# Four layers of cross attention on one core: in the narrow layer, products issued for two key tiles at a time, with sixteen probability buffers

## The reference

```python
xn = rmsnorm(x, norm_w)
q = (xn @ wq).reshape(B, T, N_HEADS, HEAD_DIM)        # 16 heads of width 16
k = (cond @ wk).reshape(B, S, N_KV_HEADS, HEAD_DIM)   # 4 groups share keys and values
v = (cond @ wv).reshape(B, S, N_KV_HEADS, HEAD_DIM)
scores = jnp.einsum('btgrd,bsgd->bgrts', qg, k) * scale
attn = jax.nn.softmax(scores.astype(jnp.float32), axis=-1).astype(q.dtype)
out = jnp.einsum('bgrts,bsgd->btgrd', attn, v).reshape(B, T, N_HEADS * HEAD_DIM)
return residual + out @ wo
```

## Time and profile before

| | us |
|---|---|
| median of 3 runs | 5466.34 |
| lowest, highest | 5460.77, 5468.5 |
| span of the profiled execution | 5460.9 |
| TensorE busy in it | 5173.7 (95%) |
| VectorE busy | 3684.8 (67%) |
| ScalarE busy | 2245.5 (41%) |
| GpSimd busy | 2695.0 (49%) |
| score blocks of the narrow layer, L765, 832 matmuls | 335.9 |
| maxima's tiles, L744, 1024 matmuls | 415.0 |
| products, L786, 1664 matmuls | 380.8 |

### The profile page before, as it was taken

The page is one execution under the profiler, slowest core; times in us unless marked ns, Lnnn a source line. Parts: engine busy times, 40 slices in busy tenths (PEclk is TensorE's granted clock), DMA queues, the critical chain, the costliest instruction groups (busy, mean ns, idle before and its releaser), DMA issues.

```text
span 5460.9 us, 81559 instructions
## 1 busy us (share of the span) xinstructions
PE 5173.7 (95%) x21484; PEld 2708.9 (50%) x21484; DVE 3684.8 (67%) x5908; ACT 2245.5 (41%) x4042; POOL 2695.0 (49%) x2048
## 2 busy tenths in 40 slices
PE   7999999999979898987999999999989999999999
PEld 4455545554444444444455555555445455545554
DVE  6767676767667676765767666676676667676767
ACT  2433344334425455552444444344424444444443
POOL 1656565656510101011656566666625656565655
PEclk8999999999979999997999999999989999999999
DMA  2010101010020101001010101010011010101010
GB/s 72 14 27 14 27 14 27 14 27 14 14 43 15 24 16 23 16 15 26 14 26 13 26 13 26 13 26 19 8 28 24 16 26 13 26 13 26 13 26 17
DMA packets 40356, 116.57 MB, mean 21 GB/s; under 512 B 7350, under 2 KB 20150, under 8 KB 35068
## 3 DMA queue, kind: packets, MB, share of 16 engines
q1 hardware_dynamic: 39938, 112.04, 9.4%
HBM read 26.86 MB, written 2.10 MB: 5 GB/s over the span
## 4 chain that ended last, share of the span: by engine, by line
PE 82%; issue 7%; DVE 6%; DMA 2%; SPq 1%; ACT 0%; DVEq 0%; POOL 0%; ACTq 0%; POOLq 0%
PE OB L654 19%; PE SS L594 13%; PE ST L625 11%; PE ST L627 9%; PE ST L551 5%; PE ST L567 4%; PE OB L786 4%; DVE mpart L1087 4%; PE ST L765 3%; PE SS L744 3%; PE ST L572 3%; PE ST L672 3%; PE ZB L607 2%; DMA Q<-rawQ 1%; PE ZB L744 1%
## 5 line engine op out<-in xcount | busy, mean ns | idle before, releaser
L282 POOL TENSOR_TENSOR acc<-acc,P 128x512 f32<-128x512 f32 (+1 forms) x1776 | 2362.5, 1356 | 455.1 <-ACT P L934 308.8
L934 ACT ACTIVATE P<-ST 128x512 f32<-128x512 f32 (+1 forms) x2496 | 1385.5, 597 | 2012.0 <-PE ST L627 1703.7
L1087 DVE TENSOR_REDUCE mpart<-SS 128x1 f32<-128x400 f32 (+1 forms) x3072 | 1665.0, 563 | 764.1 <-PE SS L594 709.1
L654 PE MATMUL OB<-P,V 128*64 128x512 f32 (+1 forms) x4992 | 1348.0, 618 | 1.1
L594 PE MATMUL SS<-KS,Q 128*128 128x400 f32 (+1 forms) x3072 | 1171.6, 387 | 70.2 <-DVE mpart L1087 67.1
L625 PE MATMUL ST<-Q,K 128*128 128x512 f32 (+1 forms) x2496 | 1061.3, 425 | 32.9 <-issue 18.3
L594 PEld LDWEIGHTS SS<-KS,Q 128*128 128x128 f32 x3072 | 585.0, 192 | 860.0 <-DVE mpart L1087 758.5
L627 PE MATMUL ST<-Q,K 128*128 128x512 f32 (+1 forms) x2496 | 989.6, 396 | 0.0
L278 POOL TENSOR_TENSOR acc<-P 128x512 f32<-128x512 f32 x192 | 241.3, 1278 | 1410.8 <-ACT P L934 1310.8
L625 PEld LDWEIGHTS ST<-Q,K 128*128 128x128 f32 (+1 forms) x2496 | 462.8, 185 | 515.8 <-ACT P L934 348.3
L1106 DVE RECIPROCAL R<-ZB 128x64 f32<-128x64 f32 (+1 forms) x432 | 371.3, 860 | 408.9 <-PE ZB L607 408.9
(11 more groups left out here) (126 smaller groups left out, 3608.1 us busy)
## 6 DMA issues: line engine op xcount, KB each, us to landing
Q<-Q SPq DMA_DIRECT2D x48, 512.0 KB, 4.5
KS<-K SPq DMA_DIRECT2D x48, 400.5 KB, 3.8
K<-K SPq DMA_DIRECT2D x48, 400.5 KB, 5.3
Q<-Q SPq DMA_DIRECT2D x32, 256.0 KB, 4.3
wk<-in_wk SPq DMA_DIRECT2D x25, 256.0 KB, 4.4
wv<-in_wv SPq DMA_DIRECT2D x25, 256.0 KB, 4.6
Q<-rawQ SPq DMA_DIRECT2D x16, 256.0 KB, 3.8
wq<-in_wq SPq DMA_DIRECT2D x25, 128.0 KB, 4.3
```

The source lines that it names most:

```text
L282: eng.tensor_tensor(out, out, P[0:rows_of(t), u % NP, :], ALU.add).then_inc(done, raised)
L654: last = pe.matmul(OB[64 * jj:64 * jj + 64, :], V[0:k, t, 64 * b:64 * b + 64], P[0:k, (2 * s + jj) % NP, :], start=t == 0, stop=t == KT - 1)
L934: act.activation(P[0:k, u % NP, :], ST[u % 4][0:k, :], ACT.Exp, scale=SCALE).then_inc(act_p, 1)
L1087: dve.tensor_reduce(mpart[:, i // len(KCH), i % len(KCH):i % len(KCH) + 1], SS[i % 2][:, 0:w], AX.X, ALU.max).then_inc(dve_s, 1)
```

## The change

```diff
+GRUNS = (2, 2, 2, 2, 2, 3)
+GRUN_END = [sum(GRUNS[:i + 1]) - 1 for i in range(len(GRUNS))]
...
+        PX = sb("PX", [128, 7, 512])
...
-        PG = [P[:, i, :] for i in range(NP)] + [acc[:, i // 2, i % 2, :] for i in range(3)]
+        PG = [P[:, i, :] for i in range(NP)] + [acc[:, i // 2, i % 2, :] for i in range(3)] \
+            + [PX[:, i, :] for i in range(7)]
...
+                def weigh(t):
+                    k = rows_of(t)
+                    for j in range(JQ):
+                        last = pe.matmul(OB[j * QD:j * QD + QD, :], V[0:k, t, g * QD:g * QD + QD],
+                                         PG[(t * JQ + j) % len(PG)][0:k, :], start=t == 0, stop=t == KT - 1)
+                    last.then_inc(gpe_pv, 1)
...
-                    pr.wait(gact_p, GROUPS * GUNITS, h * GUNITS + JQ * (t + 1))
-                    for j in range(JQ):
-                        last = pe.matmul(OB[j * QD:j * QD + QD, :], V[0:k, t, g * QD:g * QD + QD],
-                                         PG[(t * JQ + j) % len(PG)][0:k, :], start=t == 0, stop=t == KT - 1)
-                    last.then_inc(gpe_pv, 1)
+                    if t in GRUN_END:
+                        pr.wait(gact_p, GROUPS * GUNITS, h * GUNITS + JQ * (t + 1))
+                        for r in range(t + 1 - GRUNS[GRUN_END.index(t)], t + 1):
+                            weigh(r)
...
-                        if u >= len(PG) or h > 0:
-                            v = max(u - len(PG), -1) + 1
-                            pr.wait(gpe_pv, GROUPS * KT, h * KT + -(-v // JQ))
+                        if u >= len(PG):
+                            pr.wait(gpe_pv, GROUPS * KT, h * KT + (u - len(PG)) // JQ + 1)
+                        elif h > 0:
+                            before = GUNITS - 1 - (GUNITS - 1 - u) % len(PG)
+                            pr.wait(gpe_pv, GROUPS * KT, (h - 1) * KT + before // JQ + 1)
```

More of the change, by code:

```diff
@@ L772, in group_attend @@
                 for t in range(KT):
-                    k = rows_of(t)
                     tiles = g_s_units(t) if other else []
```

## The result

The changed kernel takes 5479.73 us (median of 9 runs, 5474.16 to 5484.82) against 5464.22 for the kernel before (9 runs, 5460.77 to 5468.5): ratio 1.0026 [1.0017, 1.0036], some 14 us slower. The forecast was 5478. It was added up as +12.1 us on the median of three runs, 5466.34; over nine runs that median is 5464.22. The profiled executions span 5479.1 and 5460.9 us.

What follows compares the result with a forecast made beforehand. In the narrow layer's attention, the three-bank ring of score tiles and VectorE's reductions were taken to set the pace. Terms +19.2 - 5.2 - 11.7 + 5.5 + 4.3 = +12.1 us gave 5478.4 us, range 5455 to 5491.

Steps and rivals of the forecast that it cites:

- middle pairs: Key tiles 2-9 of 15 heads: two tiles take 7.22 us against 6.90, +19.2 us in all.
- beginnings: First key tiles of 15 heads: one run replaces two groups, later, when the pace is back; -5.2 us.
- N ends: Eight DMA-bound head boundaries: transpose at 4.30, copy 8.27, next head's first score tile 12.64, 1.46 us earlier; -11.7 us.
- other seven ends: Boundaries hanging on TensorE's own chain: output copy 0.79 us later each, +5.5 us.
- last head: Head without maxima to prepare: 4.77 us per pair against 4.25, end +1.6; +4.3 us in all.
- first rival: Every removed change of tiling mode counts in full: 7 fewer per head, -52.6 us, 5414; chance 0.12.
- the ring: Three PSUM banks for maxima's score tiles, each waiting for the reduction three earlier; twelve take 4.95 us, not about 3.9.
- half pace: Head beginnings: after TensorE's wait for the queries' DMA, matmuls run at half pace; its absence would show the forecast wrong.
- second rival: The two sides cancel: run's second group costs 0.88, heads begin at full pace; +4 us, 5470; chance 0.25.
- P ends: Three head ends with query projection, among the seven where the output copy comes 0.79 us later.
- O ends: Three head ends with output projection, among the seven where the output copy comes 0.79 us later.
- third rival: Half pace spreads to the run of three: 15 heads each lose up to 1 us; 5488 or more; chance 0.13.

Runs made afterwards that it cites:

- e1: Changed kernel with all product groups single again, keeping sixteen buffers and finer waits: 0.9996 of the kernel before, 5464.91 us.
- e2: Changed kernel with runs of two only for key tiles 2-3, 4-5, 6-7 and 8-9, other products single: 1.0035 of the kernel before, 5487.1 us.
- e5: Kernel before with the maxima's reductions over 200 of 400 keys, leaving out part of the work: 0.9912 of the kernel before, 5419.56 us.
- e6: Changed kernel with the maxima's reductions over 200 of 400 keys, leaving out part of the work: 0.9875 of the kernel before, 5399.15 us.
- e3: Changed kernel with single products except the run of three at a head's end: 0.9985 of the kernel before, 5457.39 us.
- e7: Changed kernel with single products in the last head alone: 1.0009 of the kernel before, 5470.76 us.
- e9: e4 without its run of two at key tiles 0-1: 0.997 of the kernel before, 5448.39 us.
- e4: Changed kernel with runs only at tiles 0-1 and 10-11, maxima's transpose before tile 11's products, last head single: 0.9951 of the kernel before, 5439.82 us.
- e8: Kernel before with only the maxima's transpose moved ahead of key tile 11's products: 0.9981 of the kernel before, 5456.14 us.

## Why the prediction was right, step by step

| term of the sum | forecast | measured |
|---|---|---|
| middle pairs | +19.2 | 15 x 1.17 = +17.6 |
| beginnings | -5.2 | 8 x -1.11 + 7 x -0.21 = -10.3 |
| N ends | -11.7 | 8 x -1.55 = -12.4 |
| other seven ends | +5.5 | 3x0.94 + 3x1.82 + 0.82 = +9.1 |
| last head | +4.3 | +5.1 |
| buffers, waits | 0 | 0 (e1: -1.8, within its interval) |
| attention | +12.1 | +9.1 |

**Middle.** Every step of the pair came out within 0.04 us, and e2 shows it alone. The run's second group took 2.23 - 1.37 = 0.86 us. From S to S the run is 0.51 us shorter than two groups, and the twelve S take 4.97 us where two times six took 2x2.08 = 4.16, 0.81 longer: together the +0.30. The first rival (every change of mode in full, 5414) fell by e2, and what the prediction held against it is shown by e5 with e6: only with the reductions shortened to 0.37 us did merging gain in the middle. Its price was too high as well. The 0.47 us per removed group counted the step between two S, which stays; e6 has 0.21 us per pair of groups. At that price the rival's sum would be 7 x 16 x 0.21 = 24 us, not 52.6. The Trainium skill, page TensorEngine Tiling (Array Packing), section Key Properties, has it that a change of tiling mode drains TensorE. The runs show what merging two groups saves, 0.21 us where the ring lets it through; that a drain is what it saves, none of them shows.

**N ends.** Right in mechanism and size, as the three offsets above show.

**Beginnings: mis-sized, half of what they gave, and with the wrong cause.** I kept the half pace at the beginnings and named its absence as a sign of being wrong. It is absent: before, all eight heads behind an N end begin with a slow stretch; after, seven of the eight have none in their first eleven S. Their start fell from 8.47 to 7.36 us, that of the others only from 7.96 to 7.75. e3, with no run at the beginning, has the former at 7.22, so the earlier first S does it, not the pair. In the other seven heads e3 is at 8.36, so there the pair is worth some 0.6 us, and without it part of the gain would have been lost again. The shorter pause and the clock that stays up behind it are the second rival's second half ("5.2 grows to 12"), and it was right beside the forecast. One head behind an N end, head 10, begins slowly (8.19 us) with the clock up: the output copy of head 9 was late (below), and its reciprocal held the first reduction until 2179.5, 2.5 us behind its S. The attention came out at +9.1, between that rival (+4) and the forecast (+12.1).

**Other ends: too low by 3.6 us.** P ends and the last boundary came as computed (+0.94, +0.82 for 0.79). The O ends are +1.65, +1.43 and +2.38. In the second and third the run of three stands in a slow stretch, here for instance (start us, us), with the window over it:

```profile
2104.48 1.06 PE L775 MATMUL OB<-acc,V 128*32 128x512 f32 x1 [0.93 <-ACT P L1003]
...
2109.03 0.60 ACT L886 ACTIVATE Oraw<-OB 128x512 f32<-128x512 f32 x1 [4.60 <-PE OB L775]
```

```profile
2104.30:2107.80 3.50, 3.32 (x16) 0.79 (x20) 0.00 (x0) 0.13 (x1) 0.00 (x0) 0.51 0.01 2
```

The copy waits 4.60 us for the products instead of 2.98: 1.6 us late. In e7 the same boundary behind head 12 without a slow stretch took 26.32 us, +0.86 over before (0.79 forecast). So the third rival's mechanism exists, in 3 of 15 heads (8, 9 and 12), and costs 1.6 to 1.7 us in each, some 5 us in all, not 10 or more. The first O end has no slow stretch on its run. There the copy and the projection come 0.91 us later, as behind the same three heads in e3, where no run is slow. The other 0.75 us lie behind the projection, in SP's copies of the next queries, of which the third took longer to issue, before and after:

```profile
1895.33 1.45 SPq L391 DMA_DIRECT2D Q<-Q  x1
```

```profile
1896.37 2.73 SPq L395 DMA_DIRECT2D Q<-Q  x1
```

From the last addition to the next S the three O ends took 8.44, 9.43 and 7.76 us before and 9.19, 8.32 and 7.54 after, so this part varies by itself; why, no run shows.

**Last head.** The end was right (+1.6). The pair took 4.93 for 4.77, which makes five pairs +3.4, not +2.6: the first exponential starts 0.53 us behind the first score, not 0.43, and the products begin 3.08 behind it. (The "about 33.5" that I gave as its length doesn't follow from my own term; 30.78 + 4.3 is 35.1, and 35.84 was measured.)

**The total.** The ratio puts the change at +9 to +20 us, about +14; attention accounts for +9.1, and I can't trace the remainder to anything changed. In the other runs timed and attention's difference are apart by -4 to +5 us in the same way. e1 leaves the buffers at most 3 us. Three things helped the forecast of the total beyond its working: beginnings that gave 5 us more and other ends that took 4 us more nearly cancel, the rest of the program adds some 5 us that the change doesn't explain, and the median of three runs on which it stood was 2.1 us high. The mechanism in the middle and at N ends was right; that 5478 fell within 2 us of 5479.73 is luck.

## What to carry to other kernels

Before merging work on one engine to save its overhead, lay the stretch that becomes longer beside the buffers that feed the next engine: if three buffers bound it, the merge moves the idle time to the other engine and adds to it. Merge, if at all, where that engine waits anyway (here the first tiles of a head, 0.50 us between e9 and e4, part of it the clock's), and leave single what covers another engine's work (here the last head). When pricing a merge from a gap in the trace, take off the step that will stay in its place. And read what a run of instructions brings by the order that it changes: here one transpose ahead of products that it never needed gave 10 of the 27 us that e4 gained, which e8 shows in two moved lines.

## What the chip showed that I had not expected

- The pace behind a pause. Before, TensorE was idle 3.1 to 3.8 us ahead of the first S of the eight heads behind N ends, and all of them began with a stretch at half the clock (0.68 in the mean of the window). After, it was idle at most 1.5 us (0.83 in the head shown), and seven of the eight stayed at 1.00. In e8 the pause is 2.2 to 2.6 us and all eight begin slow, for a shorter time (0.77 in the mean of the first eleven S). In e4 it is 1.7 to 1.8 us in seven; four of these begin slow and three don't. In the head shown the slow stretch starts 1.8 us behind the first S:

```profile
2262.40:2264.20 1.80, 1.79 (x8) 1.36 (x9) 1.80 (x4) 1.07 (x3) 1.00 (x1) 1.00 0.00 0
2264.20:2267.60 3.40, 3.40 (x10) 2.89 (x10) 3.00 (x6) 2.47 (x6) 3.17 (x4) 0.50 0.02 5
```

- Slow stretches went from the beginnings and came elsewhere: none of the kernel before lies on the products at a head's end, three of the changed one do, and there twelve products at 0.51 cost 1.6 us. TensorE is idle 0.9 us ahead of this run in heads with and without one; what decides between them stays open.
- At half clock VectorE is no longer what holds the ring: reductions in e4 then follow S after S, each with 0.18 us idle ahead of it, at 0.76 us instead of 0.48. A head that begins slow loses 0.28 us on each S:

```profile
2266.24 0.57 DVE L1229 TENSOR_REDUCE mpart<-SS 128x1 f32<-128x400 f32 x1 [0.18 <-PE SS L754]
...
2267.00 0.57 DVE L1229 TENSOR_REDUCE mpart<-SS 128x1 f32<-128x400 f32 x1 [0.18 <-PE SS L754]
```
